# A decoder layer on one core: turns on VectorE in the last group of heads, tile 7's deviations on two engines, and the last sum by halves

## The reference

```python
x = x + attn(layernorm(x))          # 32 query heads, 8 key/value heads, head size 128, causal
x = x + cross(ctx, ctx, layernorm(x))   # per batch: softmax over keys of ctx @ query, times ctx
x = x + ffn(layernorm(x))           # 4-bit weights, groups of 128; silu(gate) * up, then down
```

## Time and profile before

| | us |
|---|---|
| median of 3 runs | 724.83 (724.61 to 726.72) |
| the profiled execution's own time | 724.8 |
| its span in the trace | 723.0 |
| busy: TensorE, VectorE, ScalarE, GpSimd | 705.2, 617.4, 384.8, 397.9 |
| last group of heads, by the timeline | about 501.5 to 569 |
| cross-attention and third norm of the last tiles | about 566 to 592 |
| feed-forward | about 581 to 719 |

### The profile page before, as it was taken

The page is one execution under the profiler, slowest core; times in us unless marked ns, Lnnn a source line. Parts: engine busy times, 40 slices in busy tenths (PEclk is TensorE's granted clock), DMA queues, the critical chain, the costliest instruction groups (busy, mean ns, idle before and its releaser), DMA issues.

```text
span 723.0 us, 11410 instructions
## 1 busy us (share of the span) xinstructions
PE 705.2 (98%) x3450; PEld 586.2 (81%) x3450; DVE 617.4 (85%) x1387; ACT 384.8 (53%) x966; POOL 397.9 (55%) x376
## 2 busy tenths in 40 slices
PE   8999999999999999999999999999999889999995
PEld 8888888888888888888888888888877657888874
DVE  6589888988898898889888988988378888898897
ACT  4566535635562655365455636563556555655643
POOL 4375536545463655266445626561445535789886
PEclk9999999999999999999999999999999999999998
DMA  9523036105701550251046003402900002322103
GB/s 299 173 72 106 1 120 218 41 0 146 225 8 30 172 167 0 94 183 52 0 116 201 2 8 98 148 0 71 338 14 0 1 1 58 88 58 67 30 12 116
DMA packets 44902, 63.92 MB, mean 88 GB/s; under 512 B 4462, under 2 KB 23278, under 8 KB 44878
## 3 DMA queue, kind: packets, MB, share of 16 engines
q1 hardware_dynamic: 44878, 63.62, 28.3%
HBM read 52.67 MB, written 10.95 MB: 88 GB/s over the span
## 4 chain that ended last, share of the span: by engine, by line
PE 88%; DVE 5%; POOL 2%; ACT 2%; issue 2%; POOLq 0%; DVEq 0%; ACTq 0%
PE psum L500 21%; PE psum L499 21%; PE psum L501 21%; PE psum L630 8%; PE psum L716 5%; PE psum L717 5%; PE psum L739 2%; PE psum L738 2%; PE psum L526 1%; DVE stats L1288 1%; ACT probs L919 1%; PE psum L505 1%; POOL o_sum L1243 1%; DVE xprobs L1414 1%; DVE negmax L1492 0%
## 5 line engine op out<-in xcount | busy, mean ns | idle before, releaser
L1434 DVE STREAM_TRANSPOSE pt<-probs 32x128 f32<-32x128 f32 x560 | 168.9, 302 | 9.1 <-POOL pt_lo L1191 2.3
L1175 POOL TENSOR_TENSOR probs<-probs,rowinv 128x512 f32<-128x512 f32 x64 | 76.5, 1195 | 156.0 <-DVE rowinv L1498 156.0
L919 ACT ACTIVATE probs<-probs,negmax 128x128 f32<-128x128 f32 x256 | 99.9, 392 | 116.0 <-DVE negmax L1492 116.0
L499 PE MATMUL psum<-xt_hi,wq_hi 128*128 128x512 f32 x256 | 102.7, 401 | 0.0
L499 PE MATMUL psum<-wo_hi,at_hi 128*128 128x512 f32 x256 | 100.2, 392 | 0.5 <-DVE at_lo L1503 0.5
L501 PE MATMUL psum<-xt_hi,wq_lo 128*128 128x512 f32 x256 | 99.8, 390 | 0.0
L500 PE MATMUL psum<-xt_lo,wq_hi 128*128 128x512 f32 x256 | 99.8, 390 | 0.0
L501 PE MATMUL psum<-wo_hi,at_lo 128*128 128x512 f32 x256 | 99.6, 389 | 0.0
L500 PE MATMUL psum<-wo_lo,at_hi 128*128 128x512 f32 x256 | 99.6, 389 | 0.0
L1191 POOL TENSOR_TENSOR pt_lo<-pt,pt_hi 128x512 fp32r<-128x512 f32 x56 | 72.4, 1293 | 24.2 <-ACT pt_hi L982 24.1
L630 PEld LDWEIGHTS psum<-kt,qt 128*128 128x128 f32 x512 | 66.8, 191 | 6.5 <-issue 1.4
(11 more groups left out here) (158 smaller groups left out, 1576.2 us busy)
## 6 DMA issues: line engine op xcount, KB each, us to landing
wq_raw<-in_L_attn_w_q SPq DMA_DIRECT2D x8, 1024.0 KB, 5.6
wo_raw<-in_L_attn_w_o SPq DMA_DIRECT2D x8, 1024.0 KB, 7.8
u_zn<-zeros_gu SPq DMA_DIRECT2D x16, 344.0 KB, 6.3
unpacked_w<-u_q SPq DMA_DIRECT2D x8, 688.0 KB, 7.8
gw<-unpacked_w SPq DMA_DIRECT2D x20, 256.0 KB, 3.5
unpacked_w<-u_q SPq DMA_DIRECT2D x6, 512.0 KB, 6.7
u_q<-in_L_ffn_gate_qweight SPq DMA_DIRECT2D x8, 344.0 KB, 5.7
u_q<-in_L_ffn_up_qweight SPq DMA_DIRECT2D x8, 344.0 KB, 4.1
```

The costliest lines, as they stand in the source:

```text
L499: pe.matmul(dst, a_hi, b_hi, start=start, stop=False)
L919: e = act.activation(probs[:, t % 2, j, :], probs[:, t % 2, j, :], ACT.Exp, bias=negmax[:, t % 2, j:j + 1], accum_out=rowsum[:, t % 2, j:j ...
L1175: pool.tensor_tensor(probs[:, t % 2], probs[:, t % 2], rowinv[:, t % 2, :].unsqueeze(2).to_broadcast([P, HG, P]), ALU.mult).then_inc(prob_ ...
L1434: turned = dve.transpose(pt[keys, :, queries], probs[queries, t % 2, :, keys])
```

## The change

Three places are edited.

In the last group, VectorE turns the probabilities of tiles 0 and 1 (LAST_BLOCKS = 2) as in the loop, with pt_lo on GpSimd, and the values of the second half of the tiles (6 block transposes in slot 1, 10 in slot 2), rounded by ScalarE at the start of slot 3, with v_lo on GpSimd. TensorE's turns begin with tile 2, in slot 3, behind fill 5. out_heads stands ahead of values in slots 2 and 3.

For tile 7, both inverse deviations are made by VectorE (the variance with eps, late_epsilon, and three steps, late_deviation) and GpSimd (the power, late_pow). TensorE turns the queries of tile 7 ahead of cross_output(5), ScalarE makes the second norm of tile 7 ahead of third(3), and VectorE takes third_second(3) behind cross_inverse(6).

At the end, GpSimd's sum of the last but one block for j = 0 is made by halves of the columns, each followed by its half of o16, and VectorE adds the first tile to xacc ahead of its last half-sum.

```diff
--- before.py
+++ after.py
@@ -53,7 +53,9 @@
     LAST_FILL = {0: [0, 1], 1: [2, 3], 2: [4], 3: [5]}
-    LAST_TURN_V = 1
+    LAST_BLOCKS = 2
+    LAST_TURN_V = {1: (0, 6), 2: (6, 16)}
+    LAST_SPLIT_V = 3
     LAST_SLOTS = NB + 1
...
@@ -595,7 +600,7 @@
                     else:
-                        pe.wait_ge(vt_lo, NG * NH)
+                        pe.wait_ge(vt_lo, NG * NH - 1)
                     turn_tile(BK_XT, xn[:, b % 2, :]).then_inc(ln_turned[1], 1)
...
             def cross_output(b):
@@ -675,25 +680,27 @@
                         scores(LAST, t)
-                    if t >= 1:
+                    if t == LAST_BLOCKS + 1:
+                        for i in LAST_FILL[t]:
+                            fill(LAST, i)
+                    if t > LAST_BLOCKS:
                         u = t - 1
-                        if u == 0:
+                        if u == LAST_BLOCKS:
                             pe.wait_ge(o_added, step + PRIME)
...
                         mm.then_inc(pt_done, 1)
-                    if t == LAST_TURN_V:
-                        turn_values(LAST, 1)
-                    for i in LAST_FILL.get(t, ()):
-                        fill(LAST, i)
+                    if t != LAST_BLOCKS + 1:
+                        for i in LAST_FILL.get(t, ()):
+                            fill(LAST, i)
                     cross_scores(t - AT_SIM)
-                    if t >= EARLY:
+                    if t >= EARLY or 2 <= t <= LAST_BLOCKS + 1:
                         out_heads(LAST, t - 2)
...
                         values(LAST, t - 1)
-                    if 2 <= t < EARLY:
+                    if LAST_BLOCKS + 1 < t < EARLY:
                         out_heads(LAST, t - 2)
...
@@ -753,8 +760,8 @@
             cross_scores(6)
+            turn_queries(7)
             cross_output(5)
-            turn_queries(7)
             cross_scores(7)
...
@@ -991,15 +998,18 @@
                         u = t - 1
-                        act.wait_ge(pt_done, u + 1 + PRIME)
+                        if u < LAST_BLOCKS:
+                            act.wait_ge(pt_turned, step + u + 1)
+                        else:
+                            act.wait_ge(pt_done, u - LAST_BLOCKS + 1 + PRIME)
                         act.wait_ge(pv_done, step + u + PRIME)
-                        act.copy(pt_hi[:], psum[:, BK_T, :].rearrange("p (a b) -> p a b", a=HG)
-                                 ).then_inc(pthi_ready, 1)
+                        act.copy(pt_hi[:], pt[:] if u < LAST_BLOCKS else
+                                 psum[:, BK_T, :].rearrange("p (a b) -> p a b", a=HG)).then_inc(pthi_ready, 1)
+                    if t == LAST_SPLIT_V:
+                        values_rounded(LAST, 1)
                     third_norm(t - AT_NORM3)
...
                         exponentials(LAST, t)
-                    if t == LAST_TURN_V:
-                        values_first(LAST, 1)
                     for i in LAST_FILL.get(t, ()):
...
@@ -1028,8 +1038,8 @@
             cross_exp(5)
+            second_norm(7)
             third(3)
-            second_norm(7)
             cross_exp(6)
...
@@ -1094,7 +1104,7 @@
             act.wait_ge(last_done, NH * HC)
-            act.wait_ge(o_summed, SUMS_BEFORE + 2)
+            act.wait_ge(o_summed, SUMS_BEFORE + 3)
             act.mul(o_part[:, 0, HALF:T], psum[:, NH * HC - 1, :], d_s[:, HC - 1, NT - 1:NT]).then_inc(last_part, 1)
...
@@ -1176,19 +1186,27 @@
+            def values_second(g, n):
+
+                half = slice(n * BH, (n + 1) * BH)
+                pool.wait_ge(vt_hi, g * NH + (3 - n))
+                pool.tensor_tensor(v_lo[:, half, :], v_raw[:], v_hi[:, half, :].bitcast(F32),
+                                   ALU.subtract).then_inc(vt_lo, 1)
+
+            def probs_second(g, u):
+
+                pool.wait_ge(pthi_ready, g * NB + u + 1)
+                pool.tensor_tensor(pt_lo[:], pt[:], pt_hi[:].bitcast(F32), ALU.subtract).then_inc(ptlo_ready, 1)
+
             def group(g):
...
                     if t in SPLIT_V:
-                        half = slice(SPLIT_V[t] * BH, (SPLIT_V[t] + 1) * BH)
-                        pool.wait_ge(vt_hi, g * NH + (3 - SPLIT_V[t]))
-                        pool.tensor_tensor(v_lo[:, half, :], v_raw[:], v_hi[:, half, :].bitcast(F32),
-                                           ALU.subtract).then_inc(vt_lo, 1)
+                        values_second(g, SPLIT_V[t])
                     if t < NB:
...
                     if TURN <= t < NB + TURN:
-                        pool.wait_ge(pthi_ready, g * NB + t - TURN + 1)
-                        pool.tensor_tensor(pt_lo[:], pt[:], pt_hi[:].bitcast(F32), ALU.subtract).then_inc(ptlo_ready, 1)
+                        probs_second(g, t - TURN)
                     for unit in SPLIT.get(t, ()):
...
@@ -1196,6 +1214,10 @@
             def last_group():
...
                 for t in range(LAST_SLOTS):
+                    if 1 <= t <= LAST_BLOCKS:
+                        probs_second(LAST, t - 1)
+                    if t == LAST_SPLIT_V:
+                        values_second(LAST, 1)
                     if t < NB:
...
@@ -1215,9 +1237,15 @@
             last_group()
-            inverse_deviation(7, 1)
-            for b in range(4, NB):
+            def late_pow(i):
+                b = NB - 1
+                pool.wait_ge(late_eps, i + 1)
+                pool.tensor_tensor(rstd[:, b:b + 1], vareps[:, b:b + 1], halfneg[:], ALU.pow).then_inc(late_power, 1)
+
+            late_pow(0)
+            for b in range(4, NB - 1):
                 inverse_deviation(b, 2)
+            late_pow(1)
             def inner(n):
...
@@ -1254,11 +1282,14 @@
             down_sum(NT - LAG - 1, HC - 1)
-            down_sum(NT - LAG, 0)
             for h in range(NH):
                 cols = slice(h * HALF, (h + 1) * HALF)
+                done, count = copied(NT, d_at(NT - LAG, 0))
+                pool.wait_ge(done, count)
+                pool.wait_ge(o_summed, 2 * (NT - LAG - 2) + 1)
+                pool.tensor_tensor(o_sum[:, 0, cols], o_part[:, 0, cols], o_sum[:, 0, cols], ALU.add).then_inc(o_summed, 1)
                 pool.wait_ge(last_part, h + 1)
-                pool.wait_ge(o_summed, SUMS_BEFORE + 2)
+                pool.wait_ge(o_summed, SUMS_BEFORE + 2 + h)
                 pool.tensor_tensor(o16[:, 0, cols], o_part[:, 1, cols], o_sum[:, 0, cols],
...
@@ -1535,9 +1566,14 @@
                     if t < NB:
-                        dve.wait_ge(pt_done, t - 1 + PRIME)
+                        if 2 <= t < LAST_BLOCKS + 2:
+                            dve.wait_ge(pt_turned, step + t - 1)
+                        elif t >= LAST_BLOCKS + 2:
+                            dve.wait_ge(pt_done, t - 1 - LAST_BLOCKS + PRIME)
                         mask(LAST, t)
-                    if t >= 1:
+                    if t in LAST_TURN_V:
+                        turn_values(LAST, 1, *LAST_TURN_V[t])
+                    if t > LAST_BLOCKS:
                         u = t - 1
...
@@ -1557,8 +1593,8 @@
                             heads_count(LAST, t - 2)
-                    if t == LAST_TURN_V:
-                        values_second(LAST, 1)
+                    if t < LAST_BLOCKS:
+                        turn_probs(LAST, t)
                     if t >= 1:
...
@@ -1587,15 +1623,35 @@
+            def late_epsilon(k):
+                r = slice(NB - 1, NB)
+                dve.wait_ge(var_ready[k], NB)
+                dve.tensor_scalar(vareps[:, r], meanvar[:, NB - 1, 1:2], EPS, 1.0, ALU.add, ALU.mult).then_inc(late_eps, 1)
+                dve.tensor_scalar(newton[:, r], meanvar[:, NB - 1, 1:2], EPS, -0.5, ALU.add, ALU.mult).then_inc(late_step, 1)
+
+            def late_deviation(i):
+                b = NB - 1
+                r, n = rstd[:, b:b + 1], newton[:, b:b + 1]
+                dve.wait_ge(late_step, 3 * i + 1)
+                dve.wait_ge(late_power, i + 1)
+                dve.tensor_scalar(n, n, r, r, ALU.mult, ALU.mult).then_inc(late_step, 1)
+                dve.wait_ge(late_step, 3 * i + 2)
+                dve.tensor_scalar(r, n, 1.5, r, ALU.add, ALU.mult).then_inc(late_step, 1)
+                dve.wait_ge(late_step, 3 * i + 3)
+                dve.tensor_scalar(shift[:, b:b + 1], meanvar[:, b, 0:1], r, -1.0, ALU.mult,
+                                  ALU.mult).then_inc(rstd_ready[i + 1], 1)
+
             cross_add(4)
...
             heads_count(LAST, NB - 1)
+            late_epsilon(1)
             cross_max(5)
+            late_deviation(0)
             cross_inverse(5)
-            third_second(3)
             cross_max(6)
             cross_inverse(6)
+            third_second(3)
             cross_add(5)
...
@@ -1604,7 +1660,9 @@
             cross_count(7)
+            late_epsilon(2)
             third_second(4)
+            late_deviation(1)
             dve.wait_ge(scales_ready, 3)
...
@@ -1673,17 +1731,18 @@
-            def last_adds(h):
```

(10 more changed lines are left out.)

3 lines of the change are left out of this document (added).

## The result

| | before | after |
|---|---|---|
| median | 725.0 (724.42 to 726.72, 12 runs) | 728.16 (726.87 to 729.15, 12 runs) |
| ratio, 95% interval | | 1.0035 (1.0025 to 1.0045) |
| the profiled execution, its span | 724.8, 723.0 | 727.82, 726.0 |

The change makes the kernel 3.2 us slower; the forecast was 2.1. The twelve times are not spread evenly. Six lie from 726.87 to 727.82 (mean 727.21) with a mean granted clock of 0.995 to 0.996, six from 728.51 to 729.15 (mean 728.84) with 0.993 to 0.994, and nothing lies between. The profiled execution is one of the first kind. So there are two questions: whether the shorter six are 2.1 us above the kernel before for the reasons given, and what adds 1.6 us to the other six.

A forecast was written before the change was run, and what follows sets the result against it. TensorE, busy 98% of the 723.0 us span, bounds the kernel, so slot 3's delay passes through. +1.85 + 0.0 + 0.25 = +2.1 us on 724.8 gives 726.9 us; forecast 725.5 to 728.1, whole range 724.3 to 729.2.

The forecast's parts named there:

- Part 1: Last group of heads: turn 2 behind fill 5 delays slot 3's exponentials, carried whole; +1.85 us, bounds +1.0 and +2.3.
- one chain to xn: Slot 3: xn of tile 0 follows exponentials, reciprocal, statistics, GpSimd's deviation; its first turn moves from 531.76 to 533.6.
- v_hi is 0.5 us of the path: Slot 3, ScalarE: rounding the values ahead of the exponentials adds 0.5 us to their start.
- Part 2: Tile 7's second and third norms: turn_third(7) waits for ft_lo instead of xm; 0.0 us, bounds -0.9 and +0.4.
- 0.2 us for norm 2: Tile 7's second norm: the shared way is about 0.7 us shorter, but only about 0.2 us arrive.
- Rival (b): Tile 7: VectorE's new order is harmless, 0.9 us are won, 726.0 us; chance 0.13.
- Part 3: Last sum by halves: first turns some 0.45 us sooner, last 16 turns 0.25 us later; bounds -0.2 and +0.6.
- one more dependent start: GpSimd's last sums: the second sum in two halves of about 1.25 us adds one dependent start, 0.14 us.
- Rival (c): Slot 3: TensorE's clock falls between the two stalls, 1.7 us of lost work, 728.6 us; chance 0.08.
- the stretch that kept it: At 586 to 590 in the kernel before, the clock stayed at 1.00 with 2.57 us of work in 4.00.

The follow-up runs named there:

- part 1 alone: Only the last-group edits of the change, put on the kernel before: 726.64 us, ratio 1.0026 to before.
- part 2 alone: Only the tile 7 edits of the change, put on the kernel before: 724.54 us, ratio 0.9993 to before.
- other queue: Only the tile 7 edits on the kernel before, with VectorE taking third_second(5) ahead of two first_adds: 723.71 us, ratio 0.999 to before.
- turn 2 first: The whole change, but in slot 3 TensorE's turn 2 stands ahead of fill 5 again: 726.03 us, ratio 1.0019 to before.
- part 3 alone: Only the edit making the last sum by halves, put on the kernel before: 725.19 us, ratio 0.9999 to before.

## Why the prediction was right, and where it was not

**Part 1, the mechanism: right.** Forecast +1.85 us, measured +1.96 at the first turn of xn and +1.90 at the last turns of part 1 alone. The steps, with the offset off, forecast first: scores(3) 522.4 and 522.37; turn 2 526.0 and 525.99; exponentials 527.6 to 527.7 and 527.63; VectorE's add ended 528.4 and 528.53; the idle time 2.1 and 2.09; mask 1 510.2 and 510.20; mask 2 518.2 and 518.52.

**Part 1, the account of who is last: incomplete.** I followed one chain to xn, from turn 2 over the exponentials. Two more stood beside it, and only the experiments brought them out: at_hi(2) behind the late out_heads(1), and the reciprocal of block 2 behind ten turns of values, under the cover of fill 5. That the sum is right although it left them out is luck: they ended at the same time or earlier. The claim that v_hi is 0.5 us of the path was wrong: without it, nothing is won.

**Part 2: right.** Forecast 0.0, the trace has -0.06, the median -0.6 with an interval that holds both. Turn_third(7) waited for ft_lo, not for xm, as described: with part 2 alone xm ends at 588.08, ft_lo of tile 5 at about 589.2 (forecast 589.4), and the turn starts at 589.26. Of the 0.2 us for norm 2, 0.15 shows at tile 6's turn of xm (85.45 us behind scores(0), in before 85.60). Rival (b), the harmless queue, did not come about as the change stands. With its other queue there were 0.9 us, but only 0.24 of them at tile 7, where that rival had them all; the rest lay in waits for first sums that the prediction did not name.

**Part 3: the mechanism right, a bit undersized.** Forecast: first turns 0.45 us sooner, last turns 0.25 later. In the whole change the products behind tile 7 are +1.89, the first turns +1.63, the last +2.41. Against part 1 alone the first turns are 0.27 sooner and the last 0.51 later. From the start of GpSimd's last sums to the last turns it was 8.77 us in before (707.63 to 716.40) and 8.80 with part 1 alone; it is 9.11 in the whole change (710.36 to 719.47), so 0.31 of the 0.51 is part 3's own. The other 0.20 lie ahead of its place: those sums start 208.24 us behind scores(0), with part 1 alone (709.92) 208.04; what makes that stays open. With them taken off, the first turns are 0.47 sooner, as forecast. The sum had the one more dependent start right: the new order has two (714.02 to 714.17 and 716.69 to 716.83), the old one had one. It put each half of the sum at 1.25 us, and they took 1.30 and 1.27, which is most of what it was short of.

**Rival (c), the clock: the step that failed.** I gave 0.08 to a fall of the clock between the two idle times, because 3.4 us of work in 7.2 seemed akin to the stretch that kept it, and the time it would give was 728.6 us. The longer executions have a mean of 728.84, and the fall is where that rival put it, worth 1.6 us where it said 1.7. It was a mistake to take it as yes or no. It comes in some executions and not in others, here in six of twelve, and the median of a kernel with two levels falls where their shares put it. The forecast's 726.9 fits the shorter executions (their median is 727.08). The measured median, 728.16, lies in the empty space between the two levels and just above the 728.1 up to which the forecast itself was to hold; that it comes so near owes something to the even shares. One kept clock in one trace of before was no evidence for all executions.

**What the order of slot 3 did.** With it as it was before, VectorE's turns cost nothing (0.0 us) and TensorE's 1.1 us of turns bring nothing; with two more places of VectorE's queue put right and part 2 in its other queue, the kernel is 1.7 us quicker. The traces have 1.50 at the last turns: 0.93 from part 2's queue, 0.53 from the place of the statistics and 0.04 from the rest. In none of these kernels did the 1.1 us of work taken from TensorE show as a gain. What counted was who is next to be late.

## What to carry to other kernels

When work is moved from a full engine to one with room, read the receiving queue instruction by instruction: each small step that someone waits for (a reciprocal, a statistic, a sum) and that comes to stand behind the moved work or behind a wait is a new candidate for the last one, even while a fill still hides it. Follow every input of the first idle instruction, not only the one that was last before. And where a change opens an idle time of 2 us in a busy TensorE, count with two levels of the time, and take enough executions to see them both.

## What the runs showed of the hardware

The granted clock does not follow from the program alone. Behind the same 2.09 us of idle time it was 1.00 in one execution and at half for eight products in another; behind idle times of 1.1 and 1.39 us (turn 2 first, 11 runs) no time stands out. It can fall behind shorter ones too. In the profiled execution of part 3 alone, where this stretch has the code of before, the clock falls behind tile 7, after idle times of 0.77 (at 589.42) and 0.93 us:

```profile
591.48 0.74 PE L716 MATMUL psum<-ft_hi,gw 128*128 128x512 f32 x1 [0.93 <-DVE ft_lo L1300]
592.02 0.63 PE L717 MATMUL psum<-ft_lo,gw 128*128 128x512 f32 x1
...
595.00 0.40 PE L716 MATMUL psum<-ft_hi,gw 128*128 128x512 f32 x1
```

Again it is eight products, 3.52 us instead of 1.95 (591.49 to 593.44 in before). Here most of it is made good. In before TensorE waits for VectorE's first sums a few products later (0.26 us at 594.78, and less behind it); here these waits are gone, and at the nineteenth product only 0.48 us are left (95.75 us behind scores(0), before 95.27). At the start of GpSimd's last sums it is 0.44 (206.61 against 206.17). That reading rests on one execution. The times of before fit it: four of its executions in the comparisons have a mean clock of 0.991 or 0.992, where most have 0.994 to 0.997, and they lie 0.5 to 0.6 us above the median of theirs. They were not profiled, so where their clock fell is not known. In these two traces, what a fall of the clock cost was set by the slack behind it, and behind slot 3 it was carried whole.
